# A selective scan by one state of two batches at a time, with its B and C rows broadcast from DRAM

## The reference

```python
D_MODEL, D_INNER, D_STATE, DT_RANK = (128, 256, 16, 64)
deltaA = jnp.exp(jnp.einsum('bld,dn->bldn', delta, A))
deltaB_u = (delta * u)[..., None] * Bm[:, :, None, :]
def step(h, t):
    dA_t, dBu_t, C_t = t
    h = dA_t * h + dBu_t
    return (h, jnp.einsum('bdn,bn->bd', h, C_t))
_, ys = lax.scan(step, h0, (dA, dBu, Ct))
return y + u * Dv
```

## Time and profile before

| | us |
|---|---|
| median of 3 runs | 1876.28 (1875.89 to 1877.37) |
| the profiled execution, its own time | 1875.95 |
| its span, first to last instruction | 1874.2 |
| of it: busy DVE / ACT / POOL / PE | 1287.5 / 1058.8 / 826.2 / 1547.2 |
| the scan stage, from its first instruction to the next section's | 165.4 to 780.5 |

### The profile page before, as it was taken

The page is one execution under the profiler, slowest core; times in us unless marked ns, Lnnn a source line. Parts: engine busy times, 40 slices in busy tenths (PEclk is TensorE's granted clock), DMA queues, the critical chain, the costliest instruction groups (busy, mean ns, idle before and its releaser), DMA issues. The chain is left out here.

```text
span 1874.2 us, 34158 instructions
## 1 busy us (share of the span) xinstructions
PE 1547.2 (83%) x12145; PEld 1066.3 (57%) x12146; DVE 1287.5 (69%) x2293; ACT 1058.8 (56%) x1931; POOL 826.2 (44%) x853
## 2 busy tenths in 40 slices
PE   5994788888887766766979999995589999878997
PEld 5762466565664444634657776662245444466886
DVE  7635888877888888877744447977862599565335
ACT  1355688878786666443544446664464577633442
POOL 1457766556568999257512225531600000027331
PEclk9996899999998889876989999997689999969999
DMA  4311011110100111267631114611651143031223
GB/s 141 115 61 46 24 54 36 54 54 30 49 23 26 30 30 29 68 230 184 111 62 59 59 57 73 104 35 59 151 99 57 29 70 55 16 138 56 72 80 95
DMA packets 153479, 132.20 MB, mean 71 GB/s; under 512 B 19070, under 2 KB 136984, under 8 KB 153058
## 3 DMA queue, kind: packets, MB, share of 16 engines
q1 hardware_dynamic: 140442, 106.20, 22.3%
q0 software_dynamic: 12800, 23.80, 4.9%
q10 hardware_dynamic: 72, 0.03, 0.0%
HBM read 77.12 MB, written 54.60 MB: 70 GB/s over the span
## 5 line engine op out<-in xcount | busy, mean ns | idle before, releaser
L768 POOL TENSOR_TENSOR xn_t<-xn_t,scan_du 128x512 f32<-128x512 f32 x256 | 321.4, 1274 | 154.2 <-ACT xn_t L915 105.6
L992 DVE TENSOR_TENSOR_SCAN xn_t<-banks,xn_t 128x512 f32<-128x512 f32 x256 | 311.5, 1217 | 78.3 <-ACT banks L905 42.2
L816 PE MATMUL banks<-scan_hc,ident 128*128 128x256 f32 x1024 | 294.6, 414 | 49.1 <-DVE scan_hc L998 49.1
L2445 ACT ACTIVATE att_pr<-banks 128x768 f32<-128x768 f32 (+1 forms) x256 | 234.3, 917 | 119.8 <-PE banks L2337 71.7
L905 ACT ACTIVATE banks<-delta,scan_exp_centre,a_neg 128x255 f32<-128x255 f32 x512 | 265.0, 559 | 13.9 <-DVE xn_t L992 13.3
L816 PEld LDWEIGHTS banks<-scan_hc,ident 128*128 128x128 f32 x1024 | 193.2, 206 | 109.9 <-DVE scan_hc L998 70.1
L998 DVE TENSOR_TENSOR scan_hc<-xn_t,banks 128x512 f32<-128x512 f32 x256 | 175.9, 687 | 33.0 <-PE banks L801 16.5
L1052 POOL DMA_INDIRECT disp<-xn_tok,places x128 | 136.7, 1068 | 109.3 <-issue 30.4
L2490 DVE TENSOR_REDUCE att_mb<-banks 128x4 f32<-128x1024 f32 x128 | 153.8, 1222 | 14.6 <-PE banks L2304 9.4
L2353 PE MATMUL banks<-att_pr,att_vx 128*32 128x256 f32 (+1 forms) x2048 | 153.1, 372 | 4.9 <-ACT att_ot L2450 3.5
L2486 DVE TENSOR_REDUCE att_mb<-banks 128x6 f32<-128x768 f32 x128 | 121.5, 956 | 32.8 <-PE banks L2311 30.6
(11 more groups left out here) (388 smaller groups left out, 3332.9 us busy)
## 6 DMA issues: line engine op xcount, KB each, us to landing
scan_ew<-f_packed SPq DMA_DIRECT2D x12, 578.0 KB, 4.2
q_parts<-att_p_parts SPq DMA_DIRECT2D x16, 384.0 KB, 4.1
k_parts<-att_p_parts SPq DMA_DIRECT2D x16, 384.0 KB, 6.2
att_qs<-q_parts SPq DMA_DIRECT2D x64, 96.0 KB
att_ks<-k_parts SPq DMA_DIRECT2D x64, 96.0 KB
gau_ew<-f_packed SPq DMA_DIRECT2D x8, 578.0 KB
disp<-zeros SPq DMA_DIRECT2D x1, 4608.0 KB, 15.5
att_xin<-disp SPq DMA_DIRECT2D x72, 64.0 KB, 1.8
```

Of the source, the lines that this page charges most:

```text
L768: nc.gpsimd.tensor_tensor(bu[:, i % RING], b_sb[:, q % 2], du[:, b % 2, c:c + 1, :].to_broadcast([P, 2, T]), ALU.mult).then_inc(s.bu_made, 1)
L816: ins = nc.tensor.matmul(bank(Y_BANK)[:, c, :], g.ident[:], hc[:, i % RING, n, :], start=False, stop=(i % (PAIRS * DC) == PAIRS * DC - 1 a ...
L992: v.tensor_tensor_scan(rows(h[:, i % 2]), g.ps[:, DA + i % RING, :], rows(bu[:, i % RING]), 0.0, ALU.mult, ALU.add).then_inc(s.scan_done, 1)
L2445: nc.scalar.activation(pr[:, i % RING], g.ps[:, at:at + 2, 0:W], ACT.Exp, scale=scale).then_inc(s.p_ready, 1)
```

## The change

- A pass now takes one state of two batches (512 columns: two rows of 256 steps of one state); there are again 128 passes of two units. `Y_BANK` is two banks, one for each half of the channels, 512 columns each.
- `mamba_front` makes B and C as plain float32 rows, one DVE copy for each of 8 chunks (`bc`), and SP stores them to DRAM (`bc_d`). The split into three parts, PE's spreading and ACT's copies are gone, and so are `C_BANK` and `b_sb`.
- In the scan SP loads, for each pass, one row of B and one of C, each broadcast over the 128 partitions (2 x 256 KB), into rings of four (`HELD`). `load_b(q+4)` waits for POOL's products of pass q, `load_c(q+4)` for the products with C of pass q.
- ACT's decay is one instruction of 510 columns. `bu` has four tiles, `h` three.
- The product with C reads `h` and `c_rows`, both in SBUF. For every unit with `i % 8 == 5` POOL makes it (`read_out`), placed behind the product `bu` of unit i+2.
- One matmul of 512 columns sums a unit. The skip term is a matmul with a diagonal matrix, made once by ACT. Gate, projection and take-out come once for 16 passes: the gate in two products, the projection in four pieces, one in each of passes 2 to 5.

```diff
+                def load_b(q):
+                    if q >= NQ:
+                        return
+                    b, n = divmod(q, DS)
+                    if q >= HELD:
+                        sp.wait_ge(s.bu_made, (q - HELD + 1) * DC)
+                    sp.dma_start(b_rows[:, q % HELD], bc_d[:, n, span(b)].to_broadcast([P, TT])).then_inc(b_in[q % HELD], 16)
+                def load_c(q):
...
+                    if q >= HELD:
+                        sp.wait_ge(s.hc_ready, read_by_vector((q - HELD + 1) * DC))
+                        if read_by_pool((q - HELD + 1) * DC):
+                            sp.wait_ge(s.hc_pool, read_by_pool((q - HELD + 1) * DC))
+                    sp.dma_start(c_rows[:, q % HELD], bc_d[:, DS + n, span(b)].to_broadcast([P, TT])
+                                 ).then_inc(c_in[q % HELD], 16)
...
+        def by_pool(i):
+            return i % 8 == 5
...
+                def read_out(i):
+                    q = i // DC
+                    pool.wait_ge(s.scan_done, i + 1)
+                    pool.wait_ge(c_in[q % HELD], (q // HELD + 1) * 16)
+                    if i >= RING:
+                        pool.wait_ge(s.sum_done, i - RING + 1)
+                    nc.gpsimd.tensor_tensor(hc[:, i % RING], h[:, i % 3], c_rows[:, q % HELD],
+                                            ALU.mult).then_inc(s.hc_pool, 1)
...
-                    pool.wait_ge(s.b_copied, q + 1)
+                    pool.wait_ge(b_in[q % HELD], (q // HELD + 1) * 16)
                     for c in range(DC):
                         i = q * DC + c
-                        if i >= RING:
-                            pool.wait_ge(s.scan_done, i - RING + 1)
-                        nc.gpsimd.tensor_tensor(bu[:, i % RING], b_sb[:, q % 2],
-                                                du[:, b % 2, c:c + 1, :].to_broadcast([P, 2, T]),
+                        if i >= HELD:
+                            pool.wait_ge(s.scan_done, i - HELD + 1)
+                        nc.gpsimd.tensor_tensor(bu[:, i % HELD], b_rows[:, q % HELD], du[:, b % 2, c],
                                                 ALU.mult).then_inc(s.bu_made, 1)
...
+                        if i >= 2 and by_pool(i - 2):
+                            read_out(i - 2)
...
+                    nc.tensor.matmul(g.ps[:, Y_BANK[c], :], g.ident[:], hc[:, i % RING], start=False,
+                                     stop=(q % DS == DS - 1)).then_inc(s.sum_done, 1)
...
-                    for n in range(2):
-                        state = 2 * pr + n
-                        ins = nc.scalar.activation(bank(DA + i % RING)[:, n, 1:T], delta[:, c, b * T + 1:(b + 1) * T],
-                                                   ACT.Exp, scale=a_neg[:, c, state:state + 1], bias=exp_centre[:])
-                    ins.then_inc(s.da_ready, 1)
+                    nc.scalar.activation(inner(g.ps[:, DA + i % RING, :]), inner(delta[:, c, span(b)]), ACT.Exp,
+                                         scale=a_neg[:, c, n:n + 1], bias=exp_centre[:]).then_inc(s.da_ready, 1)
...
-                    v.tensor_tensor_scan(rows(h[:, i % 2]), g.ps[:, DA + i % RING, :], rows(bu[:, i % RING]), 0.0,
+                    if i >= 3 and by_pool(i - 3):
+                        dve.wait_ge(s.hc_pool, read_by_pool(i - 2))
+                    v.tensor_tensor_scan(h[:, i % 3], g.ps[:, DA + i % RING, :], bu[:, i % HELD], 0.0,
                                          ALU.mult, ALU.add).then_inc(s.scan_done, 1)
+                    if by_pool(i):
+                        return
                     dve.wait_ge(s.scan_done, i + 1)
-                    dve.wait_ge(s.c_ready, q + 1)
+                    if c == 0 or by_pool(i - 1):
+                        dve.wait_ge(c_in[q % HELD], (q // HELD + 1) * 16)
                     if i >= RING:
                         dve.wait_ge(s.sum_done, i - RING + 1)
-                    v.tensor_tensor(hc[:, i % RING], h[:, i % 2], bank(C_BANK), ALU.mult).then_inc(s.hc_ready, 1)
+                    v.tensor_tensor(hc[:, i % RING], h[:, i % 3], c_rows[:, q % HELD], ALU.mult).then_inc(s.hc_ready, 1)
```

More of the change, by code:

```diff
@@ L366, in mamba_front @@
     NCH = N // CH
-    KBC = 3 * 2 * DS
     W = 2 * DS
@@ L609, in _, with mamba_scan @@
                 finish(NCH - 1)
[L612 to L626, removed]
+def mamba_scan(nc, g, t, u, gate_d, delta, bc_d, disp, ybuf, r, scattered, f):
+    TT = 2 * T
+    NB = N // TT
+    NQ = NB * DS
     NU = NQ * DC
-    DA, C_BANK, E0_BANK, BO, Y_BANK, E1_BANK = 0, 3, 4, 5, 6, 7
-    RING = 3
+    DA, E0_BANK, BO, E1_BANK = 0, 4, 5, 7
+    Y_BANK = (3, 6)
+    PIECES = TT // P
+    RING, HELD = 3, 4
     NE, CT = E0 - FIRST_MLP0, CAP0 // P
@@ L661, in mamba_scan, with span, inner, read_by_pool @@
         weighted, weighted_bank = (s.weighted0, s.weighted1), (E0_BANK, E1_BANK)
[L662 to L668, removed]
+        ew_in, ex_in = (s.ew_in0, s.ew_in1), (s.ex_in0, s.ex_in1)
+        b_in, c_in = (s.b_in0, s.b_in1, s.b_in2, s.b_in3), (s.c_in0, s.c_in1, s.c_in2, s.c_in3)
+        def span(b):
+            return slice(b * TT, (b + 1) * TT)
+        def inner(ap):
+            return ap.rearrange("p (k t) -> p k t", t=T)[:, :, 1:T]
+        def by_pool(i):
+            return i % 8 == 5
+        def read_by_pool(i):
+            return sum(by_pool(k) for k in range(i))
+        def read_by_vector(i):
+            return i - read_by_pool(i)
         def phase(q, offset):
@@ L731, in _, with inputs @@
                 nc.gpsimd.memset(exp_centre[:], EXP_CENTRE).then_inc(s.zeroed, 1)
[L733 to L743, removed]
+                def inputs(b, c):
+                    nc.gpsimd.tensor_tensor(du[:, b % 2, c], delta[:, c, span(b)], u[:, c, span(b)],
+                                            ALU.mult).then_inc(s.du_ready, 1)
+                def read_out(i):
[6 more added lines that the diff above has]
+                                            ALU.mult).then_inc(s.hc_pool, 1)
                 def fetch(n):
@@ L796, in spread_c, with skip_term @@
[L796 to L805 removed]
+                def skip_term(b, c):
@@ L806, in skip_term @@
                     if b >= 1:
[L807 to L810 removed]
+                        pe.wait_ge(s.yg_ready, (b - 1) * DC + c + 1)
+                    if b == 0 and c == 0:
+                        pe.wait_ge(s.skip_made, DC)
+                    nc.tensor.matmul(g.ps[:, Y_BANK[c], :], d_diag[:, c, :], u[:, c, span(b)], start=True, stop=False)
@@ new lines, in sum_states, with project @@
+                    nc.tensor.matmul(g.ps[:, Y_BANK[c], :], g.ident[:], hc[:, i % RING], start=False,
+                                     stop=(q % DS == DS - 1)).then_inc(s.sum_done, 1)
+                def project(b, k):
+                    if k == 0:
+                        pe.wait_ge(s.yg_ready, (b + 1) * DC)
+                        if b >= 1:
+                            pe.wait_ge(s.o_taken, b)
+                        if b == NB - 1:
+                            pe.wait_ge(s.combined, 2 * NGRP)
+                    out = g.ps[:, BO, k * D:(k + 1) * D]
+                    for c in range(DC):
+                        nc.tensor.matmul(out, yg[:, c, k * P:(k + 1) * P], w_out[:, c, :], start=(c == 0), stop=False)
+                    nc.tensor.matmul(out, g.ident[:], g.x[:, b * PIECES + k, :], start=False,
+                                     stop=True).then_inc(s.o_ready, 1)
@@ L1033, in _ @@
                     unit(2 * q + 1)
+                    if b >= 1 and n == 0:
+                        gated(b - 1, 1)
                     for j in combined_at(q - 1):
@@ L1041, in _ @@
                         combine(j, k)
-                gated(BATCH - 1)
+                for c in range(DC):
+                    gated(NB - 1, c)
 SCATTERED_IN_FRONT = 28
```

254 lines of the change are left out of this document (95 added, 159 removed).

## The result

The changed kernel takes 1911.62 us in the median of 4 runs (1907.15 to 1915.62), the one before 1876.82: a ratio of 1.0181 (95% interval 1.0153 to 1.0208). That is slower, outside the range given, and on the other side from the forecast.

A forecast was written before the change was run, and what follows sets the result against it. It saw DVE waiting for ACT and PE in the experts stage, POOL bounding the fetches. Terms -58 + 42 + 2 + 1 - 1.5 = -14.5 from 1875.95 gave 1862 us; range 1815 to 1897, the forecast's own 1843 to 1882.

The forecast's parts named there:

- What bounds the kernel before: Scan stage: no engine full during the experts, DVE waiting for ACT and PE; POOL the bound during the fetches.
- B: The scan's experts stage, 380.1 us before: forecast 322, a gain of 58, bounds 302 and 355.
- C: The scan's fetches stage, 175.3 us before, POOL the bound: forecast 217, so +42, bounds 187 and 230.
- The gain from ACT and PE: Experts stage: fewer ACT instructions and no PE spreading remove DVE's waits, 42.2 us for ACT and 16.3 for PE.
- The cost of two SBUF inputs: DVE's product and POOL's work wait for each other: nearly hidden in B, 31 us over 63 products in C.
- the ten `du`: POOL's extra products in B, beyond the nearly hidden ones: 1.2 us each, 12 us.
- the term for the read-out in B: `read_out` waits for a scan and POOL loses part of a window: 0.4 us a group, 8 us.
- rival 3: POOL's products in a row make DVE wait, mean 0.3 us on 141 products in B: 356, whole 1896; chance 0.2.
- the base: B without any new cost: 20.1 groups of eight units, 286 us, plus 15 for takings and gates, 302.
- The upper bound of 355 for B: Products exclude each other in full length: 16.9 us a group makes 340, and 15 for the rest.
- D: The scan's last stage, after the fetches: fewer DVE products against added gate, projection and take-out, +1 us.
- The front: The part before the scan: ACT loses five copies, but then meets PE's chain, so -1.5 us.

The follow-up runs named there:

- e5_psum_noread: Changed kernel with DVE's product reading the decays' PSUM bank instead of C rows in SBUF, and no read-outs by POOL; ratio 0.9684 to the kernel before.
- e1_psum: Changed kernel with DVE's product reading the decays' PSUM bank instead of C rows in SBUF, read-outs kept; ratio 0.9761 to the kernel before.
- e2_noread: Changed kernel with no product of C on POOL, all 256 on DVE; ratio 0.9930 to the kernel before.
- e7_split: Changed kernel without read-outs, with one POOL fetch between the two products `bu` in passes with fetches; ratio 0.9896 to the kernel before.

## Why the prediction was wrong, point by point

**What bounds the kernel before: right.** With the meetings taken out (e5_psum_noread) B is 316.5, where DVE's rhythm gave 313 without read-outs; e1_psum has 314.8 where I put 302 as the end without any cost, so this lower bound was 13 us too low. POOL's bound in C holds to a us: the 187 given for C with read-outs and no meetings came out as 186.6.

**The gain from ACT and PE: right.** DVE's wait for ACT went from 42.2 us to nothing in B.

**The cost of two SBUF inputs: right in kind and in size where no read-out stands.** Meetings without read-outs cost 28.5 us in C (e2_noread against e5_psum_noread) where the sum had 31, most of it at the fetches as forecast (85.8 us of fetches against 65.7), and 14.2 in B where it had 12 for the ten `du`; nine of DVE's products did wait for a `du`, 1.08 us each. The Trainium skill's page SBUF — State Buffer, "Who interferes with whom", says that whoever issues first, DVE or POOL (GpSimd there), holds the SBUF ports that the two share for the whole instruction, and the other fully blocks. The product of 3.53 us agrees in that DVE waits for what is under way. It differs in what comes next: DVE's product was issued 0.49 us before POOL's pair, and the pair went first.

**The step that failed** is the term for the read-out in B: "`read_out` waits for a scan and POOL loses part of a window there, say 0.4 us a group, 8 us". Against it stands what the read-outs add to the cost of the meetings: 39.4 us with them and 14.2 without, so 25.2 us, 1.25 us a group. I counted what POOL loses, and did not ask what a POOL that is late does next: it follows up at once, its instruction starts just before DVE's, and DVE's product waits for it, 43 times in B. The forecast had named this (rival 3, "POOL takes DVE's turn") and left it out of its sum. In C the read-outs cost 19.1 us where 11.3 were called sure, since with meetings POOL waits 19.9 us before them for scans that come late, and in e1_psum not at all.

Of the 32 us by which B missed (354.2 against 322), 17.2 are this term. Another 12.8 lie in the base (314.8 against 302). Some 2.5 of these are the rhythm itself (without read-outs 316.5, where 302 and the 12 us that they were to save make 314). The other 10 are a gain that was counted on: a read-out was to save DVE 0.61 us, 12 us in B, and without meetings it saved 1.7, since POOL waits for the read-out's scan and its sum (45.7 us in B of e1_psum) and is late with what DVE needs next. The last 2.2 are the `du`. In all, the sum had B 4 us shorter by the read-outs (12 saved, 8 lost), and they made it 23.6 longer.

**Rival 3 was the nearest to it.** It had DVE's product waiting 0.3 us in the mean, B 356 and the whole 1896; measured are 0.36 and 354.2, and the remaining 15 us come from C (+6), D (+5), the front (+4) and what lies behind the scan (+2), less 2 in B. Its mechanism is confirmed in part: it had DVE waiting through strings of POOL products, and in B it waited for one product at a time. It had a chance of 0.2 beside a forecast that turned, as the text said, on 0.09 us a unit.

The upper bound of 355 for B, from products that exclude each other in full length, came out within 1 us, and by luck. The same count without read-outs (8.5 x 1.27 + 8 x 0.69 = 16.3 us a group) makes 343, and e2_noread took 330.6; and in the changed kernel's B POOL was idle for 55 us, so the two were not simply filling the time by turns.

**Small terms.** D came out at +6.4 instead of +1: there I had counted no meeting, and e5_psum_noread, without them, has 36.0, which is the +1. The front came out at +2.4 instead of -1.5. The first of the last 14 scatters starts at 137.3 us against 137.5, so it is what follows: the third waits 2.33 us for ACT where it waited 0.91, and starts 0.9 us later (ACT has waited 1.64 us for `delta`), and the last twelve take 20.4 us in place of 18.9. One of these met a pair of DVE's two-input sums and took 3.28 us:

```profile
144.94 3.28 POOL L1030 DMA_INDIRECT disp<-xn_tok,places  x1 [0.31 <-issue]
145.02 2.34 DVE L570 SCALAR_TENSOR_TENSOR delta<-delta,front_e 128x1024 f32<-128x1024 f32 x2
```

The 2.3 us behind the scan were not looked into.

## What to carry to other kernels

Where DVE and POOL both run all the time, look at where the two inputs of DVE's instruction lie: moving one from PSUM to SBUF kept its own length (0.69 us) and cost this stage 82 us in waits (49 without the read-outs). An instruction given to POOL to relieve DVE must be costed by what it does to POOL's lead; a late POOL follows up at once, and then it is DVE that waits, here 43 times in one stage. When a change has several parts, price them apart: here the load of B alone was worth 41 us, and the loss lay in C's rows in SBUF and in POOL's read-outs.

## What the runs showed of the hardware that I had not expected

- One DVE product of 0.69 us took up to 5.29 us in the changed kernel. A DVE product that waited for POOL went next in 50 of 51 cases where it had met one of POOL's other instructions, and was passed over by one or two more products in all 30 where it had met a DMA issued by POOL or the product straight behind one, and a product came next. In e7_split, where the one to come next was a fetch, DVE's product went before it in 41 cases. The runs do not show why.
- A fetch (indirect DMA on POOL) is not only held off by DVE's product, it holds it off too: the product shown above, issued 0.54 us into a fetch, ended only after that fetch and the pair behind it. With pairs broken up by fetches (e7_split) DVE's product still took 1.52 us.
- 256 broadcast loads of 256 KB (the traffic in B went from 40 to 162 GB/s) slowed no engine by an amount that matters: without them the stage was 4 us shorter of 645, and POOL's product took 1499 ns against 1500.
